# A two-layer attention and expert kernel: the set-up of layer 1 in a new order, and the null weights transposed by one product

## The reference, cut to what matters

```python
x = x + L0_xattn(layernorm(x), ctx, ctx)             # attention, 16 heads of 8
x = x + L0_ffn(layernorm(x))                         # 8 experts, top-1 with a capacity
x = x + L1_xattn(layernorm(x), ctx, mask)            # attention, 16 heads of 64, one null key and value
x = x + L1_ffn(layernorm(x))                         # gate, up and down products with quantised operands

# L1_xattn
xn, cn = _ln(x, ln1_s, ln1_b), _ln(context, lnc_s, lnc_b)
q, k, v = xn @ Wq, *split(cn @ Wkv)
k, v = concat(null_k, k), concat(null_v, v)
attn = softmax(where(mask, q @ k.T * scale, -max))
out = _ln((attn @ v) @ Wo, lno_s, lno_b)
```

## Time and profile before

| | |
|---|---|
| median of 3 runs | 951.37 us (950.8 to 953.16) |
| the profiled execution | 950.98 us |
| its span, first to last instruction | 949.3 us |
| PE busy | 858.2 us, 90% |
| DVE busy | 692.0 us, 73% |
| POOL busy | 484.3 us, 51% |
| ACT busy | 431.5 us, 45% |

### The profile page before, as it was taken

The page is one execution under the profiler, slowest core; times in us unless marked ns, Lnnn a source line. Parts: engine busy times, 40 slices in busy tenths (PEclk is TensorE's granted clock), DMA queues, the critical chain, the costliest instruction groups (busy, mean ns, idle before and its releaser), DMA issues.

```text
span 949.3 us, 28567 instructions
## 1 busy us (share of the span) xinstructions
PE 858.2 (90%) x10216; PEld 683.9 (72%) x10246; DVE 692.0 (73%) x1957; ACT 431.5 (45%) x1010; POOL 484.3 (51%) x992
## 2 busy tenths in 40 slices
PE   2998899998679997799999999999999999999973
PEld 1666566666469886587878878787888878888752
DVE  2777787888533555468888888888878888887865
ACT  1555555555225654234454544445444454544432
POOL 5454577878532223334555546455454655645241
PEclk9999999999679999899999999999999999999995
DMA  7664400000456653021121212112121211212120
GB/s 211 223 239 185 185 13 19 13 11 15 132 165 161 164 156 95 15 55 33 35 58 33 61 36 59 37 34 62 33 60 36 55 41 34 63 33 56 27 54 10
DMA packets 57982, 71.37 MB, mean 75 GB/s; under 512 B 8050, under 2 KB 34546, under 8 KB 57842
## 3 DMA queue, kind: packets, MB, share of 16 engines
q1 hardware_dynamic: 43842, 45.48, 18.7%
q10 hardware_dynamic: 11952, 19.86, 5.6%
q0 software_dynamic: 2048, 4.20, 1.5%
HBM read 45.13 MB, written 24.38 MB: 73 GB/s over the span
## 4 chain that ended last, share of the span: by engine, by line
PE 80%; DVE 10%; issue 3%; DMA 2%; ACT 2%; POOL 1%; SPq 0%; ACTq 0%; POOLq 0%; DVEq 0%
PE psum L1569 8%; PE psum L1499 7%; PE psum L1586 7%; PE psum L1548 7%; PE psum L1490 6%; PE psum L1528 6%; PE psum L853 4%; PE psum L1574 4%; PE psum L843 3%; PE psum L1597 3%; PE psum L354 3%; PE psum L359 3%; PE psum L371 2%; PE psum L1559 2%; PE psum L378 1%
## 5 line engine op out<-in xcount | busy, mean ns | idle before, releaser
L1744 ACT ACTIVATE a_pT<-psum 128x512 f32<-128x512 f32 x128 | 69.5, 594 | 54.8 <-PE psum L1574 54.8
L459 ACT ACTIVATE l_pT<-psum 128x512 f32<-128x512 f32 x128 | 72.9, 598 | 40.4 <-PE psum L359 35.4
L1499 PEld LDWEIGHTS psum<-a_cTm,a_Wk 128*128 128x128 f32 x512 | 63.5, 196 | 30.0 <-issue 27.2
L1341 POOL TENSOR_TENSOR f_hd<-f_hmc,f_wmean 128x1 f32<-128x1 f32 x32 | 6.7, 211 | 151.6 <-DVE f_hr L2002 151.6
L573 DVE TENSOR_REDUCE l_mx<-psum 128x4 bf16<-128x512 f32 x128 | 81.9, 681 | 1.2 <-PE psum L345 1.0
L1889 DVE TENSOR_REDUCE a_mxf<-psum 128x4 f32<-128x512 f32 x128 | 81.1, 674 | 1.4 <-PE psum L1559 1.4
L1569 PE MATMUL psum<-a_qT,a_kT 64*128 64x128 f32 x1024 | 75.3, 287 | 5.1 <-ACT a_v L1766 1.1
L1499 PE MATMUL psum<-a_cTm,a_Wk 128*128 128x128 f32 x512 | 74.7, 291 | 3.4 <-POOL a_cTm L1298 2.7
L1490 PEld LDWEIGHTS psum<-a_xT,a_Wq 128*128 128x128 f32 x512 | 64.5, 192 | 15.2 <-issue 14.3
L1569 PEld LDWEIGHTS psum<-a_qT,a_kT 64*128 64x128 f32 x1024 | 63.0, 190 | 14.6 <-issue 14.2
L1877 DVE TENSOR_TENSOR a_kT<-psum,a_nkm 128x512 f32<-128x512 f32 x64 | 42.5, 664 | 40.7 <-PE psum L1499 40.7
(11 more groups left out here) (298 smaller groups left out, 2211.3 us busy)
## 6 DMA issues: line engine op xcount, KB each, us to landing
sorted_x<-r_zeros ACTq DMA_DIRECT2D x12, 1408.0 KB, 5.9
a_r_all<-a_r_rows SPq DMA_DIRECT2D x64, 256.0 KB, 4.1
e_w<-in_E_W1b SPq DMA_DIRECT2D x39, 258.0 KB, 2.8
e_xt<-sorted_x SPq DMA_DIRECT2D x39, 64.0 KB, 2.4
sorted_y<-e_yt ACTq DMA_DIRECT2D x39, 64.0 KB, 2.6
a_cin<-in_ctx SPq DMA_DIRECT2D x32, 64.0 KB, 3.8
out<-f_x SPq DMA_DIRECT2D x32, 64.0 KB, 3.3
x_res<-in_x SPq DMA_DIRECT2D x1, 512.0 KB, 5.6
```

The source lines that it names most:

```text
L459: nc.scalar.activation(pT[:, k, :], tp[k], ACT.Exp, scale=SCALE).then_inc(exp_ready, 1)
L1499: last = nc.tensor.matmul(bank[:, i * S:(i + 1) * S], Wk[:, 4 * half + i, :], cTm[:, b % 2, :], start=True, stop=True)
L1744: nc.scalar.activation(pT[:, 2 * half + e, :], tp[e], ACT.Exp, scale=SCALE).then_inc(exp_ready, 1)
```

## The change

Five moves in the order of the streams and one replaced operation:

- The four mask quarters run one tile earlier (tiles 34 to 37 in place of 35 to 38), and the statistics of the first context follow the last of them, ahead of the bias addition of tile 38.
- POOL does `mask_context(0)` ahead of the wait for the stores and of the two gathers.
- PE does `weight_sums` behind the keys of block 0.
- ACT does the context copy ahead of the wait for POOL's memsets and of the exponential for `pn`.
- DVE does `first_context_norm` ahead of `weight_magnitudes`, and `norm(1)` ahead of `sn_copy(0)`.
- In each of the 32 blocks the four products L1600 become one transpose of the whole `pn`.

```diff
-            if RANKS + 3 * NG + 2 <= i < RANKS + 3 * NG + 6:
-                layer1_setup.masks(dve, i - RANKS - 3 * NG - 2)
+            if RANKS + 3 * NG + 1 <= i < RANKS + 3 * NG + 5:
+                layer1_setup.masks(dve, i - RANKS - 3 * NG - 1)
+            if i == RANKS + 3 * NG + 4:
+                layer1_setup.first_context(dve)
...
         mask_columns(0)
+        mask_context(0)
         for q in gathered["ready"]:
             g.wait_ge(*q)
         gather(0)
         gather(1)
-        mask_context(0)
         residual(0)
...
+        def first_context(self, dve):
+            slot_wait(dve, cin_ld, 0)
+            nc.vector.bn_stats(bn[:, 0, 1, :], cin[:, 0, :]).then_inc(x2_stats, 1)
+            dve.wait_ge(x2_stats, 1)
+            nc.vector.bn_aggr(mv[:, 0, 1, :], bn[:, 0, 1, :]).then_inc(x2_stats, 1)
...
-            for j in range(Q4):
-                last = nc.tensor.matmul(nullP[32 * j:32 * j + 32, :], pn[:, Q4 * j:Q4 * j + Q4, :].rearrange("p h g -> p (h g)"), ident[:],
-                                        start=True, stop=True, skip_group_check=True)
-            last.then_inc(sums_done, 1)
+            nc.tensor.transpose(nullP, pn[:].rearrange("p h g -> p (h g)"), ident[:]).then_inc(sums_done, 1)
...
         first_transpose()
-        weight_sums()
         keys(0, 0)
         keys(0, 1)
+        weight_sums()
         values(0, 0)
...
+        first_context()
         act.wait_ge(p_set, 3)
         nc.scalar.activation(pn[:].rearrange("p h g -> p (h g)"), ...
-        first_context()
         v_copy(0, 0)
...
-        first_context_stats()
+        first_context_norm()
         weight_magnitudes()
-        first_context_norm()
         k_copy(0, 0)
         k_copy(0, 1)
         weight_means()
         first_stats()
         first_norm()
         stats(1)
+        norm(1)
         sn_copy(0)
-        norm(1)
         maxima(0, 0)
```

More of the change, by code:

```diff
@@ L1840, in stats @@
             nc.vector.bn_aggr(mv[:, s, 1, :], bn[:, s, 1, :]).then_inc(x2_stats, 1)
[L1842 to L1846, removed]
         def first_context_norm():
```

## The result

The changed kernel takes 948.98 us in the median of 20 runs (945.49 to 952.8), the kernel before 951.5 in as many (949.33 to 954.8): a ratio of 0.997, 95% interval 0.9958 to 0.9982. It is 2.5 us faster, not the 7.7 that I forecast, and lies just outside my range. The profiled execution took 951.46 us, with a span of 949.7. That is no less than before's 949.3, but its first expert product starts at 274.98 where before's starts at 273.75, in a stage that the change doesn't touch. So I compare stretches, each measured from the end of the last down product of the experts (L853; 370.54 before, 371.79 after). The forecast column holds the prediction's steps, counted from the same point.

What follows compares the result with a forecast made beforehand. PE was taken to bound layer 1's loop (16.50 of 16.65 us busy a block), with a strict line through the first keys. Gains 3.6 + 0.2 + 0.4 + 3.5 = 7.7 us gave 943.5 us, range 940.3 to 948.3.

Steps and rivals of the forecast that it cites:

- The way to the keys: Change from stage 2 to stage 3: reordered set-up starts the first keys at 373.67 instead of 377.29, 3.6 us earlier.
- the gathers lose next to nothing: POOL in the set-up: gather(0) waits for stage 2's stores until 374.40, so the masked context ahead of it costs nothing.
- `norm(1)` ahead of `sn_copy(0)`: DVE in block 0: the first maxima no longer wait behind `norm(1)`; 0.2 us gained.
- The clock: Keys, values and queries of block 0: PE's shorter rest may change the granted clock; 0.4 us gained, bounds 4.6 and -1.9.
- PE's rest ahead of the keys: Set-up: PE's nearly idle time before the keys shrinks from 6.3 us to 2.6, with one transpose in it.
- The null weights: Each of 32 blocks: one transpose takes 0.33 us in place of 0.44 for four products; 0.11 a block, 3.5 us gained.
- the bound: Null weights, lower limit: if both borders cost, 0.47 a block, a loss of 0.03 each, 1 us in all.
- rival A: Null weights: the transpose is no cheaper than the four products (0.47 for 0.44); some 947.5 us; chance 0.24.
- The worked cover of DVE and of the copy behind `sums_done`: Loop blocks: what follows `sums_done` comes no later and DVE has 2.7 us left, so nothing takes PE's place.

Runs made afterwards that it cites:

- setup_only: The changed kernel with the four 32-column products for the null weights put back in place of the transpose; 947.63 us, ratio 0.9947.
- pool_move_only: The kernel before with only POOL's `mask_context(0)` moved ahead of the wait for the stores and of the gathers; 946.33 us in one execution.
- before_busy: The kernel before plus eight unused products in PE's set-up waits (four ahead of the first transpose, three ahead of the keys, one behind the first maxima products); 947.46 us.
- transpose_last: The changed kernel with the null-weight transpose moved behind `weighted(b, 1)`, ahead of the full-width keys; 955.49 us, ratio 1.004.
- early_context: `transpose_first` with the first context's statistics at tile 33 and POOL's deviation ahead of `null_keys`; 942.25 us, ratio 0.9921.
- early_busy: `early_context` plus three unused products in PE's set-up waits (ahead of the first transpose, ahead of the keys, behind the first maxima products); 938.26 us, ratio 0.986.
- kept_busy: `transpose_first` plus four unused products in PE's set-up waits; 938.88 us in the median of five executions, a sixth of 2009.49 left out; ratio 0.9873.
- transpose_first: The changed kernel with the null-weight transpose moved ahead of `weighted(b, 0)`, behind a full-width product; 943.75 us, ratio 0.9925.

## Why the prediction was wrong

- **The way to the keys: right.** 3.6 forecast, 3.3 in the changed kernel's profile, 3.6 in `setup_only`'s; `cn` took 0.49 in both, and of the 0.3 between them half is the first transpose at half clock and half POOL's deviation, 0.16 earlier in `setup_only`. That the gathers lose next to nothing (3.86, 3.94) held, but not for the reason given: I read the idle 0.7 ahead of the first gather as a wait for the stores, which had landed 1.9 before it. The gather could have started earlier, and the masked context now fills that slack, which is luck; in `pool_move_only`, where `cT` was late, the gather lost 2.1.
- **`norm(1)` ahead of `sn_copy(0)`: right.** From the transpose of x to the first maxima 4.67 became 4.41; 0.2 forecast.
- **The clock: right for this profile (0.0 for 0.4), wrong as a term.** I treated it as one number for a kernel. It differs from one execution to the next: of the changed kernel's 20, the fastest (945.49 us) had a mean granted clock of 0.971 and the slowest (952.8) one of 0.960. The two low stretches are worth some 3.5 and 1.4 us in the profiles; `before_busy` shows that the kernel before loses 3.9 us to them in the median. PE's rest ahead of the keys, too, was longer than I wrote: from the last down product it is 6.8 us before and 3.5 after, not 6.3 and 2.6.
- **The null weights: this step failed.** I wrote 0.21 + 0.11 + 0.01 = 0.33 a block. The 0.21 ahead was right (0.20). What follows it is 0.26, not 0.12: the 0.11 was read from the second of two transposes, and "a 64-column product behind a full-width one has no idle" from L1586 behind eight full-width products in a row. One full-width operation alone between column-tiled ones is another case. The row nearest to it, a transpose right behind 32-column products and ahead of 32-row ones (L299: 0.21 and 0.26), gave 0.47, and measured is 0.46. I had it as the bound (a loss of 1 us; measured 1.1) and as rival A, with a chance of 0.24. Its time, 947.5, is 1.5 off the median.
- **What hides what.** The worked cover of DVE and of the copy behind `sums_done` held, but I took it for wide. `transpose_last` shows that 1.3 us later on ACT is already more than there is.

The range ended at 948.3 because I counted rival A mostly without its loss and with the whole of the set-up's gain. The measured parts, 3.3 less 1.1, take a median of 951.5 to 949.3; measured is 948.98.

## What to carry to other kernels

Price an operation from the row in which it has the same neighbours, not from the same shape elsewhere: here one transpose cost 0.11 us beside full-width products and 0.46, with its idle, between column-tiled ones, and moving it by one group turned a loss of 1.1 us into a gain of 3.5 (508.85 us from the first copy of `nullP` to the last, against 512.39 before). Where PE waits a few us in a row, look at the granted clock of what follows: a few unused products in the wait can be worth more than a shorter wait. And when one engine does other work ahead of what the next stage needs (POOL's gathers ahead of the masked context), move that first; the rest of the new order without it gained 0.5 us of the 3.6.

## What the runs showed of the hardware

- With the two statistics steps and the wait between them ahead of it, tile 38's addition, which first loads a register (L971), started 0.7 us behind its product, with 0.64 idle put down to issue; it started 0.14 behind it where the statistics stood elsewhere (`early_context`). That the register load behind the wait is the reason is read from the order of the rows; no run takes it out alone. It cost nothing here, since `cn` waited for POOL anyway.
- The spread of the changed kernel's runs (7.3 us) is in part the clock of the first block: with PE kept busy there it was 2.4 and 2.7 us over 5 runs each (`early_busy`, `kept_busy`), against 4.9 and 7.9 over 6 (`early_context`, `transpose_first`). With the old set-up it shrank less, from 4.6 over 15 runs to 3.9 over 11 (`before_busy`).
- From tile 36's addition to tile 37's it took 1.4 to 2.6 us in the fourteen profiles, with PE idle up to 1.1 us ahead of the last up products in the slow ones and no edit that explains it. By the program it could be the load of that tile's weights; no run tested it, and it stays open.
